# Attention of an early-fusion transformer: rounding the second matrices in halves, and one copy for the second bank of turned probabilities

## The reference, cut to what matters

```
scores  = einsum('bhqd,bhkd->bhqk', Q, K) / sqrt(16)
weights = softmax(scores, axis=-1)
out     = einsum('bhqk,bhkd->bhqd', weights, V)
```

## Time and profile before

| | us |
|---|---|
| median of 3 runs | 1114.38 (1110.06 to 1118.21) |
| the profiled execution, its own time | 1115.24 |
| its span in the trace | 1113.4 |
| PE busy / PEld busy | 932.3 / 843.5 |
| DVE busy | 569.7 |
| ACT busy | 574.5 |
| POOL busy | 620.6 |

### The profile page before, as it was taken

One profiled execution on the slowest core, in us unless ns is written; L12 is line 12 of the kernel. 1 busy time (PEld: TensorE's weight loads), 2 busy tenths in 40 slices (PEclk: granted clock), 3 DMA queues, 4 the chain that ended last, 5 costly groups with the idle time before them and its releaser, 6 DMA issues. The chain is left out here.

```text
span 1113.4 us, 20955 instructions
## 1 busy us (share of the span) xinstructions
PE 932.3 (84%) x6700; PEld 843.5 (76%) x6700; DVE 569.7 (51%) x1280; ACT 574.5 (52%) x1201; POOL 620.6 (56%) x605
## 2 busy tenths in 40 slices
PE   6259699998699999969987999941699999999960
PEld 5248467776588988848886999941699999999960
DVE  1335489996555556338764465438233333333325
ACT  0021167776435656547645556630566666666640
POOL 0105658885625554435316998730477778778740
PEclk9669999998779999989997999965799999999985
DMA  7581234443011111100007000043466666666656
GB/s 250 163 296 51 65 134 149 164 147 138 1 58 58 58 58 58 58 1 1 2 1 310 1 15 24 20 180 151 143 189 195 206 194 201 193 191 200 200 154 244
DMA packets 64899, 137.04 MB, mean 123 GB/s; under 512 B 12505, under 2 KB 26578, under 8 KB 63490
## 3 DMA queue, kind: packets, MB, share of 16 engines
q1 hardware_dynamic: 55842, 113.34, 31.6%
q0 software_dynamic: 4848, 14.72, 3.8%
q10 hardware_dynamic: 4144, 8.16, 2.0%
HBM read 114.03 MB, written 24.39 MB: 124 GB/s over the span
## 5 line engine op out<-in xcount | busy, mean ns | idle before, releaser
L122 DVE CAST place<-place 128x512 fp32r<-128x512 f32 (+1 forms) x170 | 89.2, 567 | 166.8 <-PE moe_down L128 101.5
L2337 POOL TENSOR_TENSOR place<-place,place 128x512 fp32r<-128x512 f32 x84 | 138.1, 1644 | 51.5 <-DVE place L122 51.1
L2363 PE MATMUL moe_up<-place,place 128*128 128x128 f32 x1376 | 161.9, 276 | 0.0
L2363 PEld LDWEIGHTS moe_up<-place,place 128*128 128x128 f32 x1376 | 158.3, 193 | 0.0
L128 PE MATMUL moe_down<-place,place 128*128 128x256 f32 x1008 | 131.1, 286 | 0.4 <-POOL place L2337 0.4
L128 PEld LDWEIGHTS moe_down<-place,place 128*128 128x128 f32 x1008 | 123.4, 191 | 0.6 <-issue 0.6
L2422 ACT ACTIVATE place<-place 128x2048 f32 x44 | 84.0, 1912 | 43.6 <-PEq L2159 29.9
L2435 ACT ACTIVATE place<-moe_up,place 128x128 f32<-128x128 f32 x344 | 97.5, 366 | 13.5 <-POOL place L2337 13.2
L1425 POOL TENSOR_TENSOR place<-place,place 128x384 fp32r<-128x384 f32 x42 | 43.4, 1036 | 92.8 <-ACT place L1332 64.1
L787 PE MATMUL scores<-place,place 128*69 128x276 f32 x256 | 68.5, 412 | 11.1 <-DVE place L851 6.7
L1134 PE MATMUL ff_down<-place,place 128*128 128x256 f32 x486 | 70.7, 291 | 5.4 <-POOL place L1425 4.9
(11 more groups left out here) (273 smaller groups left out, 1987.2 us busy)
## 6 DMA issues: line engine op xcount, KB each, us to landing
place<-w_remainder SPq DMA_DIRECT2D x172, 256.0 KB, 3.8
place<-in_w_dram SPq DMA_DIRECT2D x4, 4096.0 KB, 13.3
place<-gate_rows SPq DMA_DIRECT2D x24, 384.0 KB, 4.8
place<-in_w_dram SPq DMA_DIRECT2D x16, 512.0 KB, 3.7
w_remainder<-place SPq DMA_DIRECT2D x16, 512.0 KB, 3.0
place<-value_rows SPq DMA_DIRECT2D x64, 64.0 KB, 2.3
place<-choices ACTq DMA_DIRECT2D x5, 768.0 KB, 8.4
place<-in_patches_dram SPq DMA_DIRECT2D x9, 384.0 KB, 4.1
```

The source lines that it names most:

```text
L122: return eng.tensor_copy(out, x)
L2337: pool.tensor_tensor(lo[f], raw[f], hi[f].bitcast(F32), ALU.subtract).then_inc(h_split, 1)
L2363: last = pe.matmul(p1[u][k // HK][:, (k % HK) * P:(k % HK + 1) * P], ws[u][:, c, k * P:(k + 1) * P], xT[u][:, c, :], start=(c == 0), stop= ...
```

## The change

The rounding of a part is done in two instructions of 128x512, one in each of two following images, where it was one of 128x1024 in every second image. `make_rest(j)` waits for both, comes one image later in GpSimd's program, and the last one stands behind its loop. The two copies out of the second bank (207 columns of 128 rows, 69 columns of 80 rows) become one of 276 columns of 128 rows. Since it also reads the 48 rows that no transpose writes, VectorE sets the bank to zero ahead of everything else in its program, and TensorE waits for that once, before the first transposes.

```diff
                 def make_rest(j):
-                    pool.wait_ge(w2_cut, j + 1)
+                    pool.wait_ge(w2_cut, 2 * j + 2)
...
-                    if n % 2 == 1:
-                        make_rest(n // 2)
+                    if n % 2 == 0 and n >= 2:
+                        make_rest(n // 2 - 1)
+                make_rest(W2 - 1)
...
                 pe.wait_ge(preset, 6)
+                pe.wait_ge(step, 1)
...
+                link(dve.memset(tp[1][:, :], 0.0))
                 link(dve.tensor_reduce(few_mask, ...
...
                     act.wait_ge(pt_mm[1], n + 1)
-                    act.activation(pt[n % 2][:, SPLIT:J], tp[1][:, 0:(J - SPLIT) * S].rearrange("p (j s) -> p j s", s=S), ACT.Copy)
-                    act.activation(pt[n % 2][0:few, J], tp[1][0:few, (J - SPLIT) * S:(J - SPLIT + 1) * S], ACT.Copy).then_inc(pt_read[1], 1)
+                    act.activation(pt[n % 2][:, SPLIT:J + 1], tp[1][:, 0:(J + 1 - SPLIT) * S].rearrange("p (j s) -> p j s", s=S),
+                                   ACT.Copy).then_inc(pt_read[1], 1)
...
-                def cut_part(j):
+                def cut_part(j, side):
                     act.wait_ge(w2_part_in[j % 2], 16 * (j // 2 + 1))
                     if j >= 2:
                         act.wait_ge(w2_rest_made, j - 1)
-                    act.activation(w2_lead[j % 2], w2_raw[j % 2], ACT.Copy).then_inc(w2_cut, 1)
+                    at = slice(side * rows // 2, (side + 1) * rows // 2)
+                    act.activation(w2_lead[j % 2][:, at], w2_raw[j % 2][:, at], ACT.Copy).then_inc(w2_cut, 1)
...
-                    if n % 2 == 0:
-                        cut_part(n // 2)
+                    cut_part(n // 2, n % 2)
                 copy_out(NB - 1)
```

More of the change, by code:

```diff
@@ L899, in copy_probs @@
                 def copy_probs(n):
-                    few = HEADS * KR
                     act.wait_ge(pt_mm[0], n + 1)
```

## The result

| | before | after |
|---|---|---|
| median | 1113.79 us (6 runs, 1110.06 to 1118.21) | 1129.89 us (6 runs, 1127.98 to 1131.88) |
| profiled execution: span | 1113.4 | 1128.3 |
| DVE busy | 569.7 | 593.5 |
| ACT busy | 574.5 | 576.1 |
| POOL busy | 620.6 | 620.3 |

The change makes the kernel slower: ratio 1.014, 95% interval 1.0117 to 1.0164, some 16 us, where 4 us of gain were forecast. VectorE has 23.8 us more busy time, with one instruction more. That is the first clue: VectorE has the same work, and its records are longer.

What follows compares the result with a forecast made beforehand. TensorE was taken as the bound, held up by ScalarE every second image. 1115.24 - 5.68 (loop) + 1.36 (end) = 1110.9 us, or 1110.1 on the runs' median; forecast 1110.6 us, range 1106 to 1116.

Steps and rivals of the forecast that it cites:

- The bound and its cause: Attention loop: TensorE is the bound, and ScalarE's rounding holds it up 0.38 us in every second image.
- The term of 5.68 us: Attention loop: 29 steps at 4.01 us take 116.29 us, 5.68 less than before.
- The two prices on ScalarE: ScalarE in the loop: a half rounding takes about 0.62 us, the single copy of 276 columns 0.39.
- VectorE: the step that failed: VectorE in the loop: 3.95 us of work a step, 4.03 with every `spread_few` at its longest; 4.01 taken.
- GpSimd: the same step: GpSimd in the loop: `make_rest` ends 4.0 us behind the transposes, masks stay ahead; cost nothing.
- The part loads and the start: SP's part loads keep 2.3 us to spare; the starting memset, 0.7 us, falls into VectorE's idle time; both cost nothing.
- The end: End of the attention block: SP's last store arrives last, and the next block's first matmul comes 1.36 us later.
- The rival of a smaller loop gain: Loop: slack at weight load or VectorE is missing, steps take about 4.08 us, total 1112.6 us; chance 0.2.
- The slower rival (late part loads): First half rounding on ScalarE: part loads come late, +8.5 us, total 1119.1 us; chance 0.05.
- The clock behind the attention: TensorE's clock in the next block shifts, saving or losing at most 2.7 us: 1108 or 1113.5 us; chance 0.1.

Runs made afterwards that it cites:

- the four versions in which `make_rest` hits nothing: Changed kernel with one-input `spread_few` (1110.01 us), GpSimd's work behind `spread_few` and `make_rest` halved (1108.68), that with two old copies (1109.91), or only `make_rest` waiting (1107.1).
- with two copies: Changed kernel with GpSimd's work begun behind `spread_few`, `make_rest` in halves, the two old copies and no memset: 1109.91 us, ratio 0.9956.
- the version kept apart: Changed kernel with GpSimd's work of each image begun behind `spread_few`, and `make_rest` in halves: 1108.68 us, ratio 0.9946.

## Why the prediction was wrong, point by point

- **The bound and its cause: right.** ScalarE's whole rounding held TensorE up by 0.38 us in every second image. With it cut, TensorE runs at 4.01: in the first four steps of the changed kernel, and in all 29 but one of the four versions in which `make_rest` hits nothing; why that one takes 4.19 (4.05 with two copies) stays open. The term of 5.68 us measured 121.97 - 116.34 = 5.63 in the version kept apart.
- **The two prices on ScalarE: right**, 0.63 and 0.394 us.
- **VectorE: the step that failed.** The prediction had `spread_few` at "412 ns in the median and 581 at the longest", so that "all at the longest add 0.08 an image". Those were not the two ends of a price but two places in time. In the kernel before it began with GpSimd idle (0.41) or some 0.3 ahead of the end of a mask (0.56):

```profile
188.86 0.41 DVE L860 TENSOR_TENSOR place<-place,place 80x256 f32<-80x256 f32 x1
...
192.09 4.53 POOL L768 TENSOR_TENSOR place<-place,place 128x552 f32<-128x552 f32 x4
...
192.93 0.56 DVE L860 TENSOR_TENSOR place<-place,place 80x256 f32<-80x256 f32 x1
```

All 14 long ones of that loop end 0.28 us behind the end of a mask. So the duration is what is left of the GpSimd instruction under way, and 0.28; with `make_rest` of 2.36 us that is an estimated 2.64 at most, and 2.52 was seen. The prediction allowed VectorE 4.03 us an image at the worst; the 29 steps averaged 4.78.
- **GpSimd: the same step.** That the masks, made three images ahead, stay ahead was right and beside the point: GpSimd is late for nobody, it is in the way. The prediction had `make_rest` begin 1.63 behind the transposes and end at 4.0. It never asked where `spread_few` stands: in the kernel before it ends 1.56 behind them (188.86 + 0.41 - 187.71), 0.07 ahead of that `make_rest`. And with masks of about 1.13 from 4.0 on, the second begins near 5.13, where the next `spread_few` comes at 4.01 + 1.15 = 5.16. Set side by side, these leave less than a tenth and less than nothing. In the kernel before, `make_rest` began 2.07 behind the transposes, 0.5 clear of it. That half a microsecond is what the change took away.
- **The part loads and the start: right.** No ScalarE rounding waits for a DMA in the loop. The memset took 0.48 us (0.7 taken) and was hidden.
- **The end: right in kind.** TensorE's next block begins 12.27 behind image 30's transposes, 11.99 forecast, 10.63 before. SP's last wait was the late one, as forecast.
- **The rivals.** The rival of a smaller loop gain, by VectorE's small reserve, named the right engine at 0.07 us an image; it was 0.77, (138.73 - 116.34) / 29. The slower rival (late part loads) had the wrong resource. The clock behind the attention moved nothing of size: the granted clock of the next block's first 5.72 us was 0.50 before and 0.57 after, and from its first matmul to the feed-forward stage it took 11.42 and 11.19 us.

The Trainium skill has the rule that I did not set against the rows (SBUF — State Buffer, Who interferes with whom): a VectorE instruction with two SBUF inputs contends with a GpSimd instruction that reads SBUF. The same section calls the contention for the shared ports an exclusive lock. The trace agrees in both directions: `spread_few` ends 0.3 us behind the end of `make_rest` at 162.04; and where both began at 286.39 us, `spread_few` took its 0.41 and `make_rest` 2.63 in place of 2.36:

```profile
286.39 0.41 DVE L862 TENSOR_TENSOR place<-place,place 80x256 f32<-80x256 f32 x1
286.39 2.63 POOL L762 TENSOR_TENSOR place<-place,place 128x1024 fp32r<-128x1024 f32 x1 [7.39 <-ACT place L929]
```

With one input it was never over 416 ns.

## What to carry to other kernels

When a duration in a profile has two values for one shape, ask what ran on the neighbouring engine at its start before using them as bounds; here the record grows and no idle time appears. Moving work on GpSimd by half a microsecond can cost more than the work moved is worth, so lay both engines' instructions on one time axis behind a common event, and where they meet either let one wait for the other or use a form with one SBUF input. A slack of a few hundredths of a microsecond on a recurring place isn't a margin, because one late instruction can lock the loop into a slower pattern that is then stable.

## What the runs showed of the hardware

- A VectorE `tensor_tensor` with both inputs in SBUF took 0.41 us for 256 columns alone and up to 2.52 when a GpSimd instruction of 2.36 had begun 0.11 us before it; with GpSimd instructions of half the size the longest was 1.41. A `tensor_reduce` with one input took 0.405, also while a mask ran, and a `tensor_tensor` with one input in PSUM took 728 to 730 ns beside masks and `make_rest` alike.
- Each `spread_few` of the changed kernel that began inside a GpSimd instruction, 26 in a row, ended 0.28 us behind the end of that instruction. The wait shows as a longer record, with no idle time and no releaser.
- A hit of 0.92 us on VectorE, once in about six images, cost nothing; the loop absorbed it.
- The feed-forward stage behind the attention varied by 4 us (190.8 to 195.1) between profiles whose code for it is the same.
